# Routed experts of a mixture-of-experts layer on 38 blocks of 128 sorted rows in place of 22 of 256

## What is computed

```python
x  = L0_attn_x                       # (2, 2048, 128), 4096 tokens
xn = layernorm(x)
out = x + attention(xn) + ffn(xn)    # gated linear attention, 16 heads of 8, and 8 experts

gates = route(xn, Wr)                # expert 0 for every token, and the best one of the other 7
for e in range(8):                   # d_model 128, d_ff 512
    h = silu(xn @ W1[e].T) * (xn @ W3[e].T)
    out_ffn += gates[:, e:e+1] * (h @ W2[e].T)
```

## Time and profile before

| what | value |
|---|---|
| median of 3 runs | 376.96 us (374.95 to 378.18) |
| profiled execution | 376.87 us, its span 375.1 us |
| PE busy | 328.8 us, 88% of the span |
| DVE, ACT, POOL busy | 265.9, 222.0, 243.5 us |
| routed stage on PE | from about 258 us to 364.5 us |
| last scatter to `out` | starts at 368.2 us |

### The profile page before, as it was taken

How to read it: one execution, slowest core, us unless ns; L and a number is a source line. 1 busy time by engine, 2 the same in 40 slices (tenths; PEclk the granted TensorE clock), 3 DMA queues, 4 the chain that set the end, 5 groups by cost and what they waited for, 6 DMA issues and landing times.

```text
span 375.1 us, 14237 instructions
## 1 busy us (share of the span) xinstructions
PE 328.8 (88%) x5226; PEld 268.0 (71%) x5226; DVE 265.9 (71%) x577; ACT 222.0 (59%) x474; POOL 243.5 (65%) x292
## 2 busy tenths in 40 slices
PE   0778899599999989999988999999399997999970
PEld 0667765266666657777777999999299996999960
DVE  4973472255999989889837899978267775777740
ACT  1444788444666656555557777666167776777750
POOL 5423041655999989999949999900047776667773
PEclk9999999656999999999999999999699999999996
DMA  8588029411343422122242111111225445344332
GB/s 223 203 278 257 0 83 181 132 37 48 106 125 106 136 65 67 47 68 72 62 147 104 31 34 36 28 42 29 58 30 74 63 61 66 51 61 64 44 37 21
DMA packets 47505, 31.68 MB, mean 84 GB/s; under 512 B 12542, under 2 KB 45182, under 8 KB 47198
## 3 DMA queue, kind: packets, MB, share of 16 engines
q1 hardware_dynamic: 39662, 22.94, 23.3%
q0 software_dynamic: 7504, 7.95, 12.0%
q10 hardware_dynamic: 288, 0.09, 0.1%
HBM read 18.17 MB, written 12.79 MB: 83 GB/s over the span
## 4 chain that ended last, share of the span: by engine, by line
PE 80%; issue 5%; ACT 4%; POOL 4%; DVE 2%; POOLq 0%; DVEq 0%; ACTq 0%
PE PS L983 77%; POOL out L551 4%; PE PS L999 2%; PE PS L1150 1%; ACT C L577 1%; DVE rows L795 1%; ACT F L697 0%; POOLq L126 0%; ACT Z L589 0%; DVE C L887 0%; ACT L697 0%; ACT L628 0%; ACT L611 0%; POOL C L517 0%; ACT C L687 0%
## 5 line engine op out<-in xcount | busy, mean ns | idle before, releaser
L551 POOL DMA_INDIRECT out<-F,ids x44 | 68.3, 1552 | 56.8 <-DVE ids L920 33.9
L983 PE MATMUL PS<-C 64*32 64x64 f32 (+3 forms) x2816 | 88.6, 278 | 4.0 <-issue 3.0
L983 PEld LDWEIGHTS PS<-C 64*32 64x32 f32 (+3 forms) x2816 | 60.7, 123 | 30.9 <-issue 17.7
L930 DVE TENSOR_TENSOR F<-F,PS 128x512 f32<-128x512 f32 x76 | 51.4, 684 | 23.8 <-PE PS L983 14.8
L983 PE MATMUL PS<-C,W 128*128 128x256 f16 (+1 forms) x530 | 63.4, 277 | 3.9 <-DVE C L924 3.7
L697 ACT ACTIVATE F<-PS 128x512 f32<-128x512 f32 x76 | 45.4, 598 | 28.1 <-PE PS L983 21.1
L983 PEld LDWEIGHTS PS<-C,W 128*128 (+1 forms) x530 | 52.2, 100 | 11.6 <-issue 4.7
L654 ACT ACTIVATE C<-PS 128x512 f32<-128x512 f32 x64 | 38.2, 597 | 30.2 <-PE PS L983 23.6
L936 DVE TENSOR_TENSOR F<-F 128x512 f16<-128x512 f32 x76 | 52.4, 707 | 4.4 <-ACT F L702 1.1
L702 ACT ACTIVATE F<-F 128x512 f16<-128x512 f32 x76 | 47.3, 630 | 11.1 <-DVE F L930 8.6
L983 PE MATMUL PS<-xh,W 128*128 (+1 forms) x256 | 44.7, 273 | 1.7 <-DVE F L930 1.3
(11 more groups left out here) (130 smaller groups left out, 569.7 us busy)
## 6 DMA issues: line engine op xcount, KB each, us to landing
F<-w SPq DMA_DIRECT2D x8, 512.0 KB
xsort<-C POOLq DMA_DIRECT2D x1, 2860.0 KB, 8.8
C<-xsort SPq DMA_DIRECT2D x22, 130.0 KB
x_sb<-x SPq DMA_DIRECT2D x8, 256.0 KB, 4.7
k_scr<-C SPq DMA_DIRECT2D x8, 256.0 KB, 2.5
C<-k_scr SPq DMA_DIRECT2D x32, 64.0 KB, 2.2
C<-elb_scr SPq DMA_DIRECT2D x32, 64.0 KB, 2.1
out<-x_sb SPq DMA_DIRECT2D x16, 128.0 KB, 1.8
```

The costliest lines, as they stand in the source:

```text
L551: pool.indirect_dma_start(out, bass.IndirectOffsetOnAxis(ap=ids[:, k:k + 1], axis=0), ysb[:, n % 2, t, :], None, compute_op=ALU.add).then_ ...
L930: dve.tensor_tensor(silu[:, half, :], silu[:, half, :], PS[:, 3 + 4 * half, :], ALU.mult).then_inc(S["f_h"], 1)
L983: return pe.matmul(out_, lhsT, rhs, start=start, stop=stop)
```

## The change

A routed block has 128 rows. There are NBLK = 32 + 7 - 1 = 38 blocks, and the fill of each expert's part is to 128. Per block: one transpose, 24 up products of 128 columns in one piece (W1, then W3, four column blocks each), 12 down products, one silu, product, hi and lo instruction of 512 columns, one `y_copy`, one scatter. `hid_hi` and `hid_lo` are used as two buffers of half the size; `xrow` and `ysb` have four buffers of one tile. The routed stage gets semaphores of its own (`r_a`, `r_b`, `r_silu`, `r_h`, `r_hi`, `r_lo`, `r_y`) with the roles of `f_a` to `f_y`.

PE's order for block n is: up of n, transpose of n + 2, down of n - 2. The loop has UNROLL = 16; a turn loads 18 experts, and behind the loop 6 more are loaded. ACT and DVE write all 38 blocks out without a loop. SP loads rows of blocks 0 to 3 ahead of w2 and those of blocks 4 and 5 ahead of the wait for the last base store; from block 6 on they follow it.

```diff
-NBLK = N0 + R - 1
-NTILE = NBLK * BT
+NBLK = TOK // P + R - 1
+NTILE = NBLK
...
-    put("fill", (BW * np.arange(NCH))[None])
+    put("fill", (P * np.arange(NCH))[None])
...
+            def load_rows(n):
+                wait(sp, S["xs_ps"], n - 3)
+                wait(sp, S["id_copied"], n - 3)
+                sp.dma_start(xrow[:, n % 4, :], xsort[n * P:(n + 1) * P, :]).then_inc(S[f"xrow_in{n % 4}"], 16)
+
+            for n in range(4):
+                load_rows(n)
...
             for n in range(N0):
+                if n == N0 - 1:
+                    load_rows(4)
+                    load_rows(5)
                 sp.wait_ge(S["dve_y"], BT * n + BT)
...
-            loop(sp, NBLK // 2, load_rows, peel=0, start=1)
+            for n in range(6, NBLK):
+                load_rows(n)
...
+                pool.indirect_dma_start(out, bass.IndirectOffsetOnAxis(ap=ids[:, n:n + 1], axis=0),
+                                        ysb[:, n % 4, :], None, compute_op=ALU.add).then_inc(S[f"y_out{n % 4}"], 16)
...
+            for n in range(NBLK):
+                gated_silu(n)
+                if n + 2 < NBLK:
+                    sorted_hi(n + 2)
+                gated_hi(n)
+                if n >= 2:
+                    y_copy(n - 2)
...
+            for n in range(NBLK):
+                if n + 2 < NBLK:
+                    row_heads(n + 2)
+                gated(n)
+                if n == 0:
+                    add_first(N0 - 1, 1)
+                if n + 2 < NBLK:
+                    sorted_lo(n + 2)
+                gated_lo(n)
...
-            def up(e, w, bank, hi, lo, blocks):
+            def up(e, w, bank, hi, lo, blocks, wide):
...
-                    last = split_product(PS[:, bank, k * BW:(k + 1) * BW], wt[0], wt[1], hi, lo)
+                    last = split_product(PS[:, bank, k * wide:(k + 1) * wide], wt[0], wt[1], hi, lo)
...
-            UNROLL = 10
-            block_expert = [pe.alloc_register(f"block_expert{k}") for k in range(UNROLL + 1)]
+            UNROLL = 16
+            block_expert = [pe.alloc_register(f"block_expert{k}") for k in range(UNROLL + 2)]
...
+            def up_routed(n, u, e):
                 pe.wait_ge(S["xs_hi"], n + 1)
                 pe.wait_ge(S["xs_lo"], n + 1)
+                if isinstance(n, int) and n < 2:
+                    pe.wait_ge(S["f_h"], 2 * N0 - 1 + n)
+                wait(pe, S["r_silu"], n - 1)
+                wait(pe, S["r_h"], n - 1)
+                for w in range(2):
+                    up(e, w, 2 + 4 * u + w, xsh[:, u, :], xsl[:, u, :], range(FB), P).then_inc(S["r_" + "ab"[w]], 1)
...
+                wait(pe, S["y_sb"], n - 1)
+                pe.wait_ge(S["r_lo"], n + 1)
+                hi, lo = [w2_sb[:, bass.ds(e - 1, 1), part].rearrange("p o f d -> p (o f) d") for part in range(2)]
+                y = PS[:, 4 + u, 0:D]
+                for f in range(FB):
+                    mm(y, act_hi[:, u, f, :], hi[:, f, :], f == 0, False)
+                    mm(y, act_lo[:, u, f, :], hi[:, f, :], False, False)
+                    last = mm(y, act_hi[:, u, f, :], lo[:, f, :], False, f == FB - 1)
+                last.then_inc(S["r_y"], 1)
...
+                e = experts_of(UNROLL * i, UNROLL + 2)
                 for v in range(UNROLL):
+                    n, u = UNROLL * i + 2 + v, v % 2
+                    up_routed(n, u, e[v + 2])
+                    turn_rows(n + 2, v % 4, UNROLL // 4 * i + 1 + v // 4)
+                    down_routed(n - 2, u, e[v])
```

More of the change, by code:

```diff
@@ L546, in _ @@
             for n in range(NBLK):
-                pool.wait_ge(S["y_sb"], BT * n + BT)
+                pool.wait_ge(S["y_sb"], n + 1)
                 pool.wait_ge(S["id_copied"], n + 1)
[L549 to L553, removed]
+                pool.indirect_dma_start(out, bass.IndirectOffsetOnAxis(ap=ids[:, n:n + 1], axis=0),
+                                        ysb[:, n % 4, :], None, compute_op=ALU.add).then_inc(S[f"y_out{n % 4}"], 16)
         @block.scalar
@@ L703, in hidden_hi, with gated_silu, gated_hi, y_copy @@
                                    silu[:, half, :], ACT.Copy).then_inc(S["f_hi"], 1)
-            def y_copy(n, u, turn):
-                act.wait_ge(S["f_y"], N0 + n + 1)
-                wait(act, S[f"y_out{u}"], 16 * BT * turn)
+            def gated_silu(n):
+                act.wait_ge(S["r_a"], n + 1)
+                if n < 2:
+                    act.wait_ge(S["f_lo"], 2 * N0 - 1 + n)
+                wait(act, S["r_lo"], n - 1)
+                act.activation(silu[:, n % 2, :], PS[:, 2 + 4 * (n % 2), :], ACT.Silu, scale=1.0 / WS
+                               ).then_inc(S["r_silu"], 1)
+            def gated_hi(n):
+                act.wait_ge(S["r_h"], n + 1)
+                if n < 2:
+                    act.wait_ge(S["f_y"], N0 - 1)
+                wait(act, S["r_y"], n - 1)
+                act.activation(act_hi[:, n % 2].rearrange("p f t -> p (f t)"), silu[:, n % 2, :], ACT.Copy
+                               ).then_inc(S["r_hi"], 1)
+            def y_copy(n):
+                act.wait_ge(S["r_y"], n + 1)
+                wait(act, S[f"y_out{n % 4}"], 16 * (n // 4))
                 act.wait_ge(S["id_copied"], n + 1)
-                for t in range(BT):
-                    act.activation(ysb[:, u, t, :], PS[:, 4 + u, t * D:(t + 1) * D], ACT.Copy,
-                                   scale=gate_sb[:, bass.ds(n * BT + t, 1)]).then_inc(S["y_sb"], 1)
+                act.activation(ysb[:, n % 4, :], PS[:, 4 + n % 2, 0:D], ACT.Copy, scale=gate_sb[:, n:n + 1]
+                               ).then_inc(S["y_sb"], 1)
             def down_hi(n):
@@ L719, in down_hi @@
                                    ACT.Copy, scale=WS).then_inc(S["w2_hi"], 1)
[L721 to L726, removed]
             act.wait_ge(S["w_lo"], NHALF)
@@ L732, in _ @@
             hidden_hi(N0 - 2, 0)
-            sorted_hi(0, 0)
+            sorted_hi(0)
             hidden_hi(N0 - 1, 1)
[L735 to L740, removed]
+            sorted_hi(1)
+            for n in range(NBLK):
[5 more added lines that the diff above has]
+                    y_copy(n - 2)
+            y_copy(NBLK - 2)
+            y_copy(NBLK - 1)
         @block.vector
@@ L969, in _ @@
                 down_lo(n - 4)
-            sorted_lo(0, 0, 0)
+            row_heads(0)
+            sorted_lo(0)
             hidden(N0 - 1, 1)
             add_first(N0 - 2, 0)
[L973 to L977, removed]
+            row_heads(1)
+            sorted_lo(1)
+            for n in range(NBLK):
[7 more added lines that the diff above has]
+                gated_lo(n)
         @block.tensor
@@ L1143, in attend, with turn_rows @@
                     step(i, b)
-            def turn_rows(n, u, turn):
-                pe.wait_ge(S[f"xrow_in{u}"], 16 * turn + 16)
+            def turn_rows(n, r, turn):
+                pe.wait_ge(S[f"xrow_in{r}"], 16 * turn + 16)
                 wait(pe, S["xs_lo"], n - 1)
-                for t in range(BT):
-                    last = pe.transpose(PS[:, u, t * P:(t + 1) * P], xrow[:, u, t, 0:D], cc("ident"))
-                last.then_inc(S["xs_ps"], 1)
-            UNROLL = 10
-            block_expert = [pe.alloc_register(f"block_expert{k}") for k in range(UNROLL + 1)]
+                pe.transpose(PS[:, r % 2, 0:P], xrow[:, r, 0:D], cc("ident")).then_inc(S["xs_ps"], 1)
+            UNROLL = 16
+            block_expert = [pe.alloc_register(f"block_expert{k}") for k in range(UNROLL + 2)]
             def experts_of(n, count):
@@ L1191, in down_routed @@
                 if isinstance(n, int) and n < 2:
[L1192 to L1195, removed]
+                    pe.wait_ge(S["dve_y"], BT * (N0 - 1 + n))
+                wait(pe, S["y_sb"], n - 1)
[7 more added lines that the diff above has]
+                last.then_inc(S["r_y"], 1)
             def attend_four(j):
```

112 lines of the change are left out of this document (54 added, 58 removed).

## The result

| kernel | median | spread | ratio to before |
|---|---|---|---|
| before | 377.57 us | 374.95 to 379.17, 4 runs | |
| changed | 413.01 us | 411.91 to 415.47, 4 runs | 1.0955 (95%: 1.0871 to 1.1039) |

A forecast was written before the change was run, and what follows sets the result against it. PE's array bound the kernel before; afterwards its sequencer would, at 3.55 us per 128-row block. Stage start, blocks, register loads and end summed to 408.9 us against 375.1, +33.8, giving 411 us, range 402 to 426.

The forecast's parts named there:

- first address computation of block 0: Start of the routed stage on PE's queue, put at 258.1 us in the time of the profiled execution.
- y_copy and last scatter to its end: End of the routed stage: y_copy and POOL's start 0.6 us, then the last scatter 1.55 us.
- What bounds the kernel, and the sequencer: PE's array limits before; in 128-row blocks its queue needs 3.55 us, with 24 address computations of 0.12 us, setting the pace.
- The array's term: PE's array work per routed 128-row block: 2.12 us, 81 us for 38 blocks, saving 11 us on the array alone.
- array-bound rival: Routed blocks take 2.12 to 2.2 us because PE's queue works ahead or addresses serve several slices; about 358 us, chance 0.05.
- Expert numbers: PE's register loads grow to 2, 18, 18, 6 registers; loads of 18 put at 1.95 and 3.7 us, 6 at 0.92.
- a longest TENSOR_LOAD over 2.7 us: Sign that the prediction is right: PE's longest load of expert numbers into registers exceeds 2.7 us.
- Row loads: Blocks 2 to 5 requested before the last base store; PE's 5.76 us wait and the low clock behind it go.
- the 8.2 us: Cost of the hole before block 2's up products, idle PE plus low clock, which earlier row loads would remove.
- A stay at the low level behind the second load: Granted clock at half level for some 7 us at most behind the second expert load; +1.4 us, inside the range.
- rival of a low clock for most of the stage: Clock at half level over the routed stage, blocks array-bound at 4.24 us, 26 us more, about 437 us; chance 0.08.
- ACT, DVE, POOL: ACT and DVE's longest loop, at most 2.3 us, and POOL's 1.85 us per scatter, all hidden under 3.55 us per block.

The follow-up runs named there:

- a_addr16: Changed kernel with the down products' weight slice at a fixed expert, leaving 16 address computations per block; output not the reference's; 380.27 us.
- a_static: Changed kernel with fixed experts in both products, no register loads and no address computations; output not the reference's; 354.46 us, ratio to before 0.9445.
- a_addr8: Changed kernel with the up products' weight slices at a fixed expert, leaving 8 address computations per block; output not the reference's; 357.67 us.
- a_offset: Changed kernel with the list of the blocks' experts moved up by 2 words in SBUF, nothing else changed; 418.87 us.
- b_rows: Kernel before with the row loads of blocks 2 and 3 issued ahead of the wait for the last base store; 373.29 us, ratio 0.9887.
- a_down1: Changed kernel with the down products one block behind instead of two, same output; 415.17 us.
- b_best2: b_best with block 2's row load one base store earlier and experts loaded 4 at a time from multiples of 4, last piece 2; 366.74 us.
- b_best: b_rows with all 22 blocks' experts loaded in four pieces during the first expert's last products, PE's routed blocks without a loop; 367.84 us.

## Why the prediction was right, point by point

The sum against the profiled execution:

| term | put at | measured | difference |
|---|---|---|---|
| first address computation of block 0 | 258.1 | 255.9 | -2.2 |
| from there to the first load of 18 | 5.1 | 4.9 | -0.2 |
| first load of 18 and copies | 2.35 | 2.6 | +0.3 |
| 16 blocks | 56.8 | 57.9 | +1.1 |
| second load and copies | 4.1 | 2.4 | -1.7 |
| 16 blocks | 56.8 | 58.0 | +1.2 |
| loop exit, third load | 1.3 | 1.5 | +0.2 |
| four blocks, two down groups, drain | 16.9 | 17.2 | +0.3 |
| y_copy and last scatter to its end | 2.15 | 3.6 | +1.5 |
| to the end of the span | 5.3 | 6.1 | +0.8 |
| end | 408.9 | 410.3 | +1.4 |

The path is the one forecast, but that the end came out within 1.4 us is in part luck: three terms are 4.1 us too long in the sum and the others some 5.4 too short, and they nearly cancel. The largest, 2.2 us at the start, belongs to the execution and not to the change.

- **What bounds the kernel, and the sequencer.** Right. The pace of 0.12 us per computation could be read from one starved block, and the steady blocks of a_addr16 returned it. The block was put at 3.55 and is 3.62 to 3.63 in the mean over 16; 3.6, from the measured block, was the better of the two estimates.
- **The array's term.** 2.12 us per block was right, and a_static shows it at work: 2.13 per block. The 358 us given to the array-bound rival, which keeps the register loads, are to be held against the 357.7 of a_addr8.
- **Expert numbers.** The first load was sized well (1.95, measured 1.89). The second was put at 3.7 and took 1.60: the 2.74 us of the earlier trace rows goes with its start at entry 10, off a multiple of 4 words, as a_offset makes likely, whose loads of 18 from such a start took 4.53 and 4.29, and the new loop starts at 16. The named sign "a longest TENSOR_LOAD over 2.7 us" did not appear. The two loads of 18 cost 105 and 89 ns per register in the changed kernel, and 252 and 238 when they start off a multiple of 4 (a_offset).
- **Row loads.** In the changed kernel the wait is gone. How much it brings was misjudged in the small: the 8.2 us count the low clock (granted 0.50 from 266.0 to 272.7, where 24 up products took 4.51 us in place of 2.78), and in b_rows it followed shorter gaps too (0.50 for 6.8 us behind gaps of 1.03 and 1.68). In the changed kernel the gap left at this place, of the first load of 18, kept the full clock (granted 1.00 from 263.6 to 270):

```profile
263.61 2.22 PE L1014 MATMUL PS<-C,W 128*128 128x128 f16 x24 [2.43 <-issue]
```

- **The clock.** A stay at the low level behind the second load came as forecast, for 3.4 us where at most 7 or so were named:

```profile
320.00:324.40 4.40, 2.09 (x23) 1.48 (x21) 1.71 (x5) 1.16 (x3) 2.40 (x2) 1.00 0.24 30
324.40:327.80 3.40, 3.40 (x33) 3.24 (x32) 0.89 (x2) 0.87 (x2) 0.10 (x1) 0.51 0.23 24
327.80:340.00 12.20, 11.86 (x132) 9.12 (x130) 5.89 (x18) 6.30 (x15) 5.12 (x4) 1.00 0.27 41
```

  The gap was 2.31 us, almost that of the kernel before, where the granted clock stayed at 1.00. The rival of a low clock for most of the stage did not come (granted 1.00 from 270 to 320 and from 330 to 384), with the array at work for about 2.1 of 3.6 us.
- **ACT, DVE, POOL.** Hidden, as said, but for the end. There the last three down groups begin at 396.5, 397.6 and 399.3 with no up products between them, faster than POOL can scatter, and its last three scatters start 1.92 and 1.85 us apart:

```profile
398.85 1.61 POOL L556 DMA_INDIRECT out<-F,ids  x1 [1.80 <-ACT F L729]
400.77 1.55 POOL L556 DMA_INDIRECT out<-F,ids  x1 [0.30 <-issue]
402.62 1.55 POOL L556 DMA_INDIRECT out<-F,ids  x1 [0.30 <-issue]
```

  The sum let the last scatter start as if POOL were free and came out 1.5 us short there.
- **The start.** 2.2 us came from an earlier stage that the change doesn't touch. Its place is a longer or shorter stay at the low clock around 68 to 92 us; the windows 66 to 92 of the kernel before and of the changed one:

```profile
66.00:92.00 26.00, 22.61 (x326) 13.35 (x326) 10.91 (x23) 10.46 (x24) 16.43 (x26) 0.54 0.27 75
```

```profile
66.00:92.00 26.00, 22.21 (x411) 13.34 (x411) 12.62 (x27) 12.40 (x28) 17.33 (x27) 0.67 0.29 78
```

  a_static and a_down1 begin their routed stage at 258.2 and 258.4, a_addr16 and b_rows at 255.9, so this comes and goes with the run and not with the change. (In a_down1 the window 66 to 92 is at 0.67 too, but the clock dipped a second time, to a mean of 0.97 over 104 to 160.)

What the halving of the blocks could have brought is seen in a_static and a_addr8: 357.7 us with 8 computations. The rows saved are real, 4864 in place of 5632, but the address computations went from 22 x 24 to 38 x 24. No kernel here reaches this time with each block's own experts: whether addresses could be computed once and kept is open.

## What to carry to other kernels

An engine's busy share says nothing about its sequencer: PE was busy for 88% of the span before and 89% after, while its block went from 4.19 us per 256 rows to 3.62 per 128. Where instructions take their addresses from registers, count the computations per block, find a stretch in which nothing is queued on the array and read their pace there, and compare it with the array's time for the same block before making the blocks smaller: the edge here lay between 8 and 16 computations for 2.12 us of products, and between 24 and 32 for 4.19 us. Put register loads where the queue has a lead, in whole groups of four words that start at a multiple of four, as these were the quickest here (4 registers in 0.33 us in b_best2; 5 from entry 17 in 1.24 in b_best); a_offset shows what a bad start costs when nothing hides it (5.9 us), while b_best and b_best2, whose loads are hidden, differ by less than can be measured.

## What the runs showed of the hardware

- One address computation and the products behind it hold PE's queue for 0.124 us, although it is busy for 46 ns, and whether one or two products follow (starts of the changed kernel's up group, 282.28 to 283.68). It was paid only where the queue then needed longer than the array: with 8 or none of them a block of 128 rows took 2.13 us (a_addr8, a_static), with 16 it took 2.67 (a_addr16).
- A register load from SBUF takes 0.33 us for 4 words from an entry divisible by 4 (b_best2; 0.52 for the first of them), 1.60 to 1.89 for 18, but 4.3 to 4.5 for 18 that start two words further (a_offset). 2 registers took 0.72 us at either place.
- The granted clock fell to 0.50 or 0.51 of full speed behind gaps of 1.03 and 1.68 us in a row (b_rows), and behind single ones of 1.74 and 2.39 (a_addr16), 2.24 (b_rows) and 2.31 us (changed kernel). It stayed at 1.00 over gaps of 1.63 and 1.75 (a_addr8), of 2.29 and of 2.43 (changed kernel, at the first load of 18). In these runs a gap of this length cost the low clock or did not, and its length alone does not tell which. What decides is left open.
